# Products for two key blocks in a row, bias products over 128 rows, and constants in nine pieces

## What is computed

```python
def _L1_ffn_ref(x, gate_query, log_temp, w1, b1, w2, b2):
    ...
    gates, idx = jax.lax.top_k(affinity, CAP)              # 64 rows of each batch for each of 16 experts
    expert_in = jnp.take_along_axis(x[:, None, :, :], idx[..., None], axis=2)
    h = jax.nn.gelu(jnp.einsum('becd,edf->becf', expert_in, w1) + b1[None, :, None, :])
    expert_out = jnp.einsum('becf,efd->becd', h, w2) + b2[None, :, None, :]
    ...
def _L1_attn_ref(x, qW, qb, kW, kb, vW, vb, oW, ob, J):
    ...
    scores = jnp.einsum('bthd,bshd->bhts', q_, k_) * scale
    scores = scores + jnp.mean(jnp.sin(J[:T])) * 0.1
    attn = jax.nn.softmax(scores, axis=-1)
    out = jnp.einsum('bhts,bshd->bthd', attn, v_).reshape(B, T, D)
    return quat_linear(out, oW, ob)
```

## Time and profile before

| what | us |
|---|---|
| median of 3 runs | 3152.6 (3152.53 to 3155.25) |
| the profiled execution | 3154.0 |
| its span | 3152.3 |
| first loop of `Ffn1`, 1955 to 2190: TensorE, VectorE, ScalarE, GpSimd busy | 219, 170, 161, 118 |
| attention loop, 2240 to 2856 | 604, 281, 504, 18 |
| second loop of `Ffn1`, 2931 to 3145 | 212, 160, 155, 88 |
| whole span: TensorE, VectorE, ScalarE, GpSimd busy | 2777, 1814, 1651, 610 |

### The profile page before, as it was taken

How to read it: one execution, slowest core, us unless ns; L and a number is a source line. 1 busy time by engine, 2 the same in 40 slices (tenths; PEclk the granted TensorE clock), 3 DMA queues, 4 the chain that set the end, 5 groups by cost and what they waited for, 6 DMA issues and landing times.

```text
span 3152.3 us, 52924 instructions
## 1 busy us (share of the span) xinstructions
PE 2777.1 (88%) x21463; PEld 2176.5 (69%) x21463; DVE 1813.9 (58%) x3698; ACT 1650.9 (52%) x2482; POOL 610.3 (19%) x556
## 2 busy tenths in 40 slices
PE   7948999997999979669999983897899999995898
PEld 5747999996777757559999972887443444432798
DVE  6623555557887676335555567776644364435676
ACT  4413455543443444224555541676588777892676
POOL 0071021213000000620121225643100000001343
PEclk9978999999999989779999995999899999996899
DMA  5122334323000021223342343566342242423575
GB/s 175 54 92 67 109 85 96 83 72 97 2 2 2 3 51 44 99 67 101 81 100 75 80 140 101 163 181 169 84 119 51 55 122 61 110 47 108 151 199 145
DMA packets 241729, 287.23 MB, mean 91 GB/s; under 512 B 31114, under 2 KB 218726, under 8 KB 241486
## 3 DMA queue, kind: packets, MB, share of 16 engines
q1 hardware_dynamic: 205054, 226.01, 25.0%
q0 software_dynamic: 34848, 56.28, 8.7%
q10 hardware_dynamic: 1584, 1.57, 0.2%
HBM read 204.75 MB, written 87.93 MB: 93 GB/s over the span
## 4 chain that ended last, share of the span: by engine, by line
PE 72%; DVE 13%; issue 6%; ACT 4%; DMA 2%; POOL 2%; another core or an unknown queue 1%; DVEq 0%; SPq 0%; POOLq 0%; ACTq 0%
PE PS L161 16%; PE PS L162 15%; PE PS L163 15%; PE PS L2847 14%; PE PS L971 6%; DVE SM L178 1%; ACT FW L507 1%; DMA GR<-xn_scratch,SM 1%; DVE FW L585 1%; ACT Z L550 1%; DVE PROD L577 1%; PE PS L468 1%; PE PS L458 1%; PE PS L2937 1%
## 5 line engine op out<-in xcount | busy, mean ns | idle before, releaser
L161 PE MATMUL PS<-FH,FW 128*128 128x366 f32 (+1 forms) x1408 | 513.9, 365 | 61.1 <-issue 42.7
L2994 ACT ACTIVATE P<-PS 128x1024 f32<-128x1024 f32 x512 | 487.6, 1041 | 106.1 <-PE PS L2847 103.9
L163 PE MATMUL PS<-FH,FW 128*128 128x366 f32 (+1 forms) x1408 | 502.7, 357 | 21.6 <-issue 21.5
L162 PE MATMUL PS<-FH,FW 128*128 128x366 f32 (+1 forms) x1408 | 504.6, 358 | 18.5 <-issue 18.5
L501 ACT ACTIVATE FHH<-PROD 128x366 fp32r<-128x366 f32 (+1 forms) x352 | 195.7, 556 | 529.5 <-DVE PROD L577 503.2
L577 DVE TENSOR_TENSOR PROD<-SIL,PS 128x366 f32<-128x366 f32 (+1 forms) x352 | 207.1, 588 | 293.1 <-PE PS L163 171.1
L161 PE MATMUL PS<-FW,FHH 128*122 128x256 f32 (+1 forms) x1184 | 339.6, 287 | 4.4 <-issue 2.9
L163 PE MATMUL PS<-FW,FHH 128*122 128x256 f32 (+1 forms) x1184 | 334.1, 282 | 8.6 <-issue 8.6
L162 PE MATMUL PS<-FW,FHH 128*122 128x256 f32 (+1 forms) x1184 | 334.8, 283 | 3.5 <-issue 3.5
L161 PEld LDWEIGHTS PS<-FH,FW 128*128 128x128 f32 x1408 | 269.4, 191 | 97.0 <-issue 58.3
L580 DVE TENSOR_TENSOR FHH<-PROD,FHH 128x366 fp32r<-128x366 f32 (+1 forms) x352 | 209.9, 596 | 219.0 <-ACT FHH L501 214.2
(11 more groups left out here) (453 smaller groups left out, 5545.8 us busy)
## 6 DMA issues: line engine op xcount, KB each, us to landing
WS<-L_ffn_w_dram SPq DMA_DIRECT2D x256, 256.0 KB
WST<-L_ffn_W_dram SPq DMA_DIRECT2D x168, 256.0 KB
S<-parts_scratch SPq DMA_DIRECT2D x60, 384.0 KB, 7.8
parts_scratch<-PT SPq DMA_DIRECT2D x28, 512.0 KB, 4.0
Z<-xe_scratch POOLq DMA_DIRECT2D x14, 777.8 KB, 7.9
WST<-L_ffn_W1s_dram SPq DMA_DIRECT2D x40, 256.0 KB
WST<-L_ffn_W3s_dram SPq DMA_DIRECT2D x40, 256.0 KB
WST<-L_ffn_W2s_dram SPq DMA_DIRECT2D x40, 256.0 KB
```

The source lines that it names most:

```text
L161: e.matmul(o, lh, rh, start=start, stop=False, skip_group_check=True)
L162: e.matmul(o, ll, rh, start=False, stop=False, skip_group_check=True)
L163: return e.matmul(o, lh, rl, start=False, stop=stop, skip_group_check=True)
L2994: e.activation(self.PR[K % 3][:, 2 * jj:2 * jj + 2, :].rearrange("p a b -> p (a b)"), c.pair(2 * ((2 * K + jj) % 3)), ACT.Exp, scale=0.25) ...
```

## The change

It has three parts. First, `pv` is put in every second turn, for two key blocks in a row; `oc` and what follows it come a turn earlier. Second, the bias matmuls go over all 128 rows: `B2E` and `B2H` are written in full, and GpSimd clears the whole of `B2F` first. Third, the constants are cut into 16 pieces, nine of them GpSimd's, which stand one expert apart, all with the wait for scatters and gathers; those of VectorE and ScalarE come behind them, the casts (`high`) apart from the subtractions (`split`), and the two fills apart.

```diff
-    CONSTS1 = 7, 11, 15, 19, 20, 21, 22, 23, 24
+    CONSTS1 = 7, 11, 15, 19, 23, 27, 31, 35, 39, 42, 43, 45, 46, 49, 51, 54
...
-                    e.matmul(yb, self.B2E[0:48, e_:e_ + 1].broadcast_to([48, 128]), self.B2H[0:48, :], start=first,
+                    e.matmul(yb, self.B2E[:, e_:e_ + 1].broadcast_to([128, 128]), self.B2H[:, :], start=first,
                              stop=False, skip_group_check=True)
...
-            e.tensor_tensor(self.B2E[0:48, :], c.IDENT[0:48, 0:16], c.IDENT[0:48, 32:48], ALU.add)
-            e.tensor_copy(self.B2H[0:48, :], self.B2F[0:48, :]).then_inc(*p.one("dv"))
+            e.tensor_tensor(self.B2E[:, :], c.IDENT[:, 0:16], c.IDENT[:, 32:48], ALU.add)
+            e.tensor_copy(self.B2H[:, :], self.B2F[:, :]).then_inc(*p.one("dv"))
...
-            if it in self.before.items[1:5]:
+            if it in self.before.items[1:10]:
...
-            e.memset(self.B2F[0:64, :], 0.0).then_inc(*p.one("b2z"))
+            e.memset(self.B2F[:, :], 0.0).then_inc(*p.one("b2z"))
...
+    SUMS = "bvo0", "bvo1", "bvo2", "bvo3"
...
-        self.items = [("c1", k) for k in ("small", "sign", "qk", "vo", "bvo", "bi", "split", "j", "bv", "rows")]
+        self.items = [("c1", k) for k in ("small", "sign", *"qkvo", *self.SUMS, "bi", "high", "split", "j", "bv", "rows1",
+                                          "rows")]
...
-            k = K - 2
-            if k >= 0:
-                put(("pv", n, k))
-                if k % 8 == 7:
-                    self.finish(fin, put, k // 8, K)
+            if K and K % 2 == 0:
+                put(("pv", n, K - 2), ("pv", n, K - 1))
+                if K % 8 == 0:
+                    self.finish(fin, put, u - 1, K)
```

More of the change, by code:

```diff
@@ L2349 @@
     BS = ((1, -1, -1, -1), (1, 1, 1, -1), (1, -1, 1, 1), (1, 1, -1, 1))
+    SUMS = "bvo0", "bvo1", "bvo2", "bvo3"
+    MADE = {"bi": ("cv", "bi"), "qk": ("cp", "k"), "vo": ("cp", "o"), "bvo": ("cp", "bvo3"), "rows": ("cr", "rows"),
+            "sign": ("cp", "sign"), "split": ("cs", "split"), "bv": ("cv", "bv")}
     def __init__(self, chip):
@@ L2370, in __init__ @@
         self.BH = pt("BH", [128, 8], F32R)
-        self.items = [("c1", k) for k in ("small", "sign", "qk", "vo", "bvo", "bi", "split", "j", "bv", "rows")]
+        self.items = [("c1", k) for k in ("small", "sign", *"qkvo", *self.SUMS, "bi", "high", "split", "j", "bv", "rows1",
+                                          "rows")]
         counts = {"small": {"cl": 240}, "sign": {"cp": 3 + 12}, "bi": {"cv": 2}, "j": {"cv": 1, "ca": 1},
-                  "bv": {"cv": 1}, "qk": {"cp": 8}, "vo": {"cp": 8}, "bvo": {"cp": 32}, "rows": {"cr": 2},
-                  "split": {"cs": 1}}
+                  "bv": {"cv": 1}, "rows1": {"cr": 1}, "rows": {"cr": 1}, "split": {"cs": 1},
+                  **{k: {"cp": 4} for k in "qkvo"}, **{k: {"cp": 8} for k in self.SUMS}}
         for it in self.items:
-            c.p.count(it, counts[it[1]])
+            c.p.count(it, counts.get(it[1], {}))
     def stage(self):
@@ L2390, in ready @@
         for k in names:
-            w.wait_ge(*self.c.p.at({"bi": "cv", "qk": "cp", "vo": "cp", "bvo": "cp", "rows": "cr", "sign": "cp", "split": "cs",
-                                    "bv": "cv"}[k],
-                                   ("c1", k)))
+            w.wait_ge(*self.c.p.at(self.MADE[k][0], ("c1", self.MADE[k][1])))
     def pe(self, e, w, it):
@@ L2406, in act @@
             w.wait_ge(*p.at("cv", ("c1", "bv")))
-            for x in range(2):
-                dst = self.ST[x][1][:, :, :].rearrange("p j (a t) -> p (j a) t", t=128)
-                e.activation(dst, ones, ACT.Copy, scale=self.BV if x else 1.0).then_inc(*p.one("cr"))
+            x = int(k == "rows1")
+            dst = self.ST[x][1][:, :, :].rearrange("p j (a t) -> p (j a) t", t=128)
+            e.activation(dst, ones, ACT.Copy, scale=self.BV if x else 1.0).then_inc(*p.one("cr"))
     def dve(self, e, w, it):
@@ L2420, in dve @@
                 e.tensor_reduce(self.BI[x], self.BQK[:, x], AX, ALU.add).then_inc(*p.one("cv"))
-        elif k == "split":
+        elif k == "high":
             self.ready(w, "qk", "vo")
@@ L2426, in dve @@
             ins.then_inc(*p.one("dv"))
+        elif k == "split":
             w.wait_ge(*p.mine())
@@ new lines, in pool @@
+            for ci in range(4):
+                hs = slice(64 * (ci % 2), 64 * (ci % 2) + 64)
+                src = self.WL[k][hs, :, :].rearrange("p (a b) o -> p a b o", a=2)
+                if ci & 1:
+                    src = src[:, :, ::-1]
+                if ci & 2:
+                    src = src[:, ::-1]
+                w.wait_ge(*p.mine())
+                e.tensor_tensor(self.W[k][hs, ci // 2, :].rearrange("p (a b o) -> p a b o", a=2, b=2), src,
+                                self.SGM[hs, ci // 2, :].rearrange("p (a b) -> p a b", a=2).unsqueeze(
+                                    3).broadcast_to([64, 2, 2, 64]), ALU.mult).then_inc(*p.one("cp"))
+        elif k in self.SUMS:
+            x, half = divmod(self.SUMS.index(k), 2)
+            for co in (2 * half, 2 * half + 1):
+                d = self.BVO[:, x, 64 * co:64 * co + 64]
+                w.wait_ge(*p.mine())
+                e.tensor_copy(d, self.BT[x][:, 0, :]).then_inc(*p.one("cp"))
+                for q in range(1, 4):
+                    w.wait_ge(*p.mine())
+                    e.tensor_tensor(d, d, self.BT[x][:, q, :], ALU.add if self.BS[co][q] > 0 else
+                                    ALU.subtract).then_inc(*p.one("cp"))
```

25 lines of the change are left out of this document (2 added, 23 removed).

## The result

| | before | after |
|---|---|---|
| median of 20 runs each, us | 3148.6 | 3158.3 |
| ratio | | 1.0032, 95% interval 1.0023 to 1.0041 |
| the profiled execution, its span | 3154.0, 3152.3 | 3161.1, 3159.4 |
| first loop of `Ffn1`, first to last bias matmul | 219.4 | 210.8 |
| attention, first to last score matmul | 612.7 | 636.2 |

The account below looks back on a forecast made before the run. TensorE was taken to bound the expert loops, and TensorE and ScalarE in turns the attention, over three score buffers. 3154.0 - 24.5 - 5.5 + 9 = 3133, less 1.4 for the median: 3131.6 us, range 3114 to 3146.

Parts of the forecast that it names:

- Bias matmuls: Both expert loops: 128 rows instead of 48 save 0.38 us for each of 64 matmuls, 24.5 us (0 to 24.5).
- rival 2: Expert loops: the 48-row matmul isn't slow for its rows, 128 cost the same; 3156 us, no change; chance 0.10.
- what is late next: Expert loops: whether a feeding engine becomes late once experts are faster; answered that ScalarE and VectorE move forward with TensorE.
- Constants on GpSimd: First expert loop: GpSimd falls behind 10 (lower end) to 24 us, 8 of lateness free; 4 us stall (0 to 10).
- The piece `j`: First expert loop: VectorE's six steps, the sine and ScalarE's table change make TensorE wait 3.3 us again.
- The gain of 5.5 us: First expert loop: it keeps 15.1 of the 20.6 us it loses, a gain of 5.5 us (0 to 14).
- Pairs: Attention: two key blocks' P products side by side lose 9 us, bounds 15 us gained to 15 lost.
- ring: Attention: three score buffers; ScalarE starves for 0.25 us in every pair of key blocks without other work.
- The prediction's formula: Attention: a pair lasts the larger of both sums; Xe and Xo are other work in its even and odd turn.
- Rival 3: Attention: the ring starves ScalarE in busy turns too, up to 0.54 us a pair, 69 us, 3192 us; chance 0.05.
- Rival 1: Attention: the ring never holds TensorE, so the pairs gain 15 us; 3107.6 us; chance 0.20.
- Rival 4: First expert loop: GpSimd's pieces keep the gathers as late as before, the 5.5 us gain is gone; 3137; chance 0.05.

Follow-up runs that it names:

- e8: e4 with the weights of each expert's third step rounded in full by ScalarE, one VectorE subtraction replacing three instructions; 3001.7 us, ratio 0.9944 to the kernel before.
- e10: e8 with the signed sums of the biases moved from GpSimd to VectorE; 2997.4 us, ratio 0.9918 to the kernel before.
- e4: The full change without the pairs: bias matmuls over 128 rows and constants in nine pieces; 3010.5 us, ratio 0.9964 to the kernel before.
- e1: The kernel before with the bias matmuls over 128 rows and nothing else; 3012.4 us, ratio 0.9969 to the kernel before.
- e14: e6 with the transposes of the attention output one turn later; 3021.5 us, a single run.
- e3: The kernel before with the products of P and V for two key blocks side by side, nothing else; 3040.8 us, ratio 1.0071 to the kernel before.
- e6: The kernel before with pairs and exponentials over 512 of 1024 columns, so the output is not the reference's; 3026.0 us, ratio 1.0019.

## Why the prediction was wrong

Point by point, by its own steps.

**Bias matmuls, 24.5 us forecast, some 10 measured (5.1 in the second loop).** The cost itself was right: 0.38 us for each, and rival 2 falls. (64 times 0.38 is 24.3 and not 24.5, which changes nothing.) This also answers the two rules of the Trainium skill that the prediction weighed. The Trainium skill's "TensorE: Matmul & The Clock Gate", section "Step-by-step: what each phase is for", says of a weight load that its time doesn't depend on the rows. The trace agrees: the load lasts 0.18 us with 48 and with 64 rows and 0.19 with 128. The prediction took more from it than it says, that the whole matmul costs the same. What differs is when the load starts, 0.33 us behind the load before it in place of 0.12. The weight loads of the kernel before, in order of time:

```profile
2098.53 0.19 PEld L163 LDWEIGHTS PS<-XT,FW 128*128 128x128 f32 x1
2098.86 0.18 PEld L2098 LDWEIGHTS PS<-B2H,B2E 48*128 48x128 f32 x1
```

The distances fit the Trainium skill's "TensorEngine Tiling (Array Packing)", section "Key Properties", that a change of tiling mode drains the engine, if 48 and 64 rows count as another mode than 128, which no run here tests by itself. The step that failed in this part is the answer to "what is late next". I took it from shares of busy time (VectorE 170 of 235 us) and from the sentence that "a row of weights is split two steps ahead". The split is issued two steps ahead, but in the step in which VectorE also reads out the finished rows, and it takes three instructions in a row there. With an expert shorter by 0.77 us this chain ended 0.4 us too late in each expert. e8 shows it: with the split lightened by two instructions, the second loop gives the whole 12.3 us. The forecast had bounds of 0 to 24.5 for this term, but its range held it at 24.5.

**Constants on GpSimd, 4 us of stall forecast, some 10 measured.** The demand was about right: I had GpSimd fall behind by 1.3 to 3.0 us an expert, and the fifth to the eleventh expert last 0.6 to 1.8 us longer than the 12.8 of the second loop. What failed is the estimate that 8 us of lateness are free, and the choice of the lower end. TensorE waits for the gathers from the sixth expert on, 8.0 us in seven waits, and for the XT halves around them another 2.4.

**Constants on VectorE and ScalarE.** The piece `j` was sized at 3.3 us plus a part of 2. It cost 3.6 in front of the XT half, 1.3 behind it, and 2.2 for 23 matmul distances of 0.213 instead of 0.12 us from 2122.90 to 2129.41, at a granted clock of the lower of the two levels, 1.2 GHz: 7.1 us. Against the undisturbed 186.5 us of e10's second loop the first loop keeps 24.3 us instead of 15.1. That leaves some 7 us for the other pieces, which had been given 5.8, and for the waits for the split, which the traces don't divide. The gain of 5.5 us isn't shown. The first loop gained 3.5 us more than the second (8.6 against 5.1), e4's is 1.9 us shorter than e1's, and both are within the 3.8 us by which the unchanged first loop varies.

**Pairs, 9 us lost forecast, 23.5 measured (24.1 alone).** Taken apart by the distances from start to start in the two traces, in which the waits in front of other work are left out of the first two rows:

| | forecast, us | measured, us |
|---|---|---|
| distances behind P groups, 237.6 in place of 252.8 (a P block takes 1.854 in place of twice 0.996) | -15 | -15.2 |
| ring: distances behind score groups, 202.2 in place of 177.9; of it 18.0 in the 25 pairs without work in the odd turn | +24 | +24.3 |
| waits in front of the other work: its distances above the shortest of each kind, 37.0 in place of 22.2 | 0 | +14.8, of it the transposes of the output 8.0 |
| the other work at its shortest distances, 159.4 in place of 159.7 | 0 | -0.3 |
| sum | +9 | +23.6 |

The ring's term was right in size: 24 us, and a pair without other work lasts 3.90 us where 3.86 was forecast and 3.66 measured before. What failed is that the other work X was put into the formula as a constant. X waits too: for the one bank that it has, and for data that VectorE makes from the X or the P block before. Before, 1.65 us lay between the end of one turn's P block and the next X; in an odd turn after the change it is 0.66. The prediction's formula, the larger of 3.86 + Xe and 3.20 + Xe + Xo, has no term for it. And e14 shows that this term can't simply be taken off: when the transposes stopped waiting, the rest of X waited 7.9 us longer and the ring some 3 us. So the rows of the table say what TensorE waited for, not what each cause would give back.

**The rivals.** Rival 3 (slower, since the P block stands ahead of each second score group in the busy turns too, deciding from 30 us) is the one that came nearest: the side was right, the price was 24 us and not 30, and it decided already there, because half of the gain of the bias matmuls was missing. It had been given 0.05. Against it I held that in busy turns ScalarE idles anyway; but a ScalarE with idle time can still be late for the one buffer that TensorE needs next. Rival 1 fell. Rival 4 is true in its mechanism: TensorE waits for the gathers as long as before, 8.0 us over seven experts in place of 7.8 over three. The sum failed by two terms of the same sign, 14 us in the bias matmuls and 14 in the pairs; either alone would have left the kernel no slower than before. The ends of the range, 3114 and 3146 us, don't follow from the bounds that the prediction gives (constants -14 to 0, pairs -4 to +15 make 3110 and 3143), but 3158.3 is outside of both.

## What to carry to other kernels

When an edit takes time out of a loop, go through the queue of the engine that feeds it instruction by instruction at the place where its input is due, and don't read its slack from its busy share: 75% busy was late by 0.4 us in each expert. A ring of buffers doesn't ask for an even share of work but for an even spacing: two blocks side by side save 0.14 us of switching, and where nothing filled the gap a pair was still 0.24 us longer. Treat work that shares a single bank as waiting work, and give it a distance as well as a duration.

## What the runs showed of the hardware

- A matmul over 48 or 64 rows among matmuls over 128 rows costs 0.38 us more than one over 128 rows (distances of 0.21, 0.31 and 0.22 us in place of 0.12 each), though it does less and its weight load lasts no longer (0.18 and 0.19 us). Filling it up with zero rows takes that away.
- From the start of a score group over its exponential to the next score group in the same buffer it takes 0.59 us beside the exponential itself, whether that is 1.03 or 0.60 us long (e3 and e6).
- The 32 instructions over 64 columns that kept GpSimd for 15.6 us, 12.9 us of it in the instructions themselves, take VectorE 0.19 and 0.22 us each, 7.0 us in all (e10).
